# A macaron block with routed experts: quad addresses worked out together, and r projected from mixed rows

## What is computed

```python
x = x + 0.5 * ffn(layernorm(x))     # pass A
x = x + attn(layernorm(x))
x = x + 0.5 * ffn(layernorm(x))     # pass B
# ffn: shared swiglu of width 256, plus for each token the best 2 of 8 experts of width 128,
#      weighted by their normalised sigmoid scores
# attn:
xx = x shifted by one token
xk, xv, xr = (x * mix + xx * (1 - mix) for mix in (mix_k, mix_v, mix_r))
k, v, r = xk @ Wk.T, xv @ Wv.T, xr @ Wr.T
state_t = k_t * v_t + exp(time_decay) * state_(t-1)
o_t = r_t * (time_first * k_t * v_t + state_t)
out = layernorm(o) @ Wo.T
```

## Time and profile before

| | |
|---|---|
| median of 3 runs | 1294.95 us (1294.62 to 1298.04) |
| the profiled execution | 1293.77 us |
| its span, first to last instruction | 1291.5 us |
| mean granted TensorE clock | 0.916 of full speed |
| busy: TensorE, VectorE, GpSimd, ScalarE | 1042.8, 829.3, 714.7, 457.3 us |
| instructions | 28331 |

### The profile page before, as it was taken

How to read it: one execution, slowest core, us unless ns; L and a number is a source line. 1 busy time by engine, 2 the same in 40 slices (tenths; PEclk the granted TensorE clock), 3 DMA queues, 4 the chain that set the end, 5 groups by cost and what they waited for, 6 DMA issues and landing times.

```text
span 1291.5 us, 28331 instructions
## 1 busy us (share of the span) xinstructions
PE 1042.8 (81%) x8816; PEld 714.9 (55%) x8816; DVE 829.3 (64%) x2520; ACT 457.3 (35%) x819; POOL 714.7 (55%) x684
## 2 busy tenths in 40 slices
PE   1788699978898999789997979985899877698560
PEld 0466466744466666357664466755567444467450
DVE  5965668577779567766767854666576777642242
ACT  6334245422235444324432135342345223223230
POOL 2846752378873335777348781257842775530264
PEclk9989899997899999899997989997999988899795
DMA  9869985443375654469743577679744533477794
GB/s 289 222 122 211 243 163 131 98 121 98 119 151 104 164 128 144 142 142 211 168 136 110 163 149 171 155 205 183 181 107 132 143 110 90 118 154 170 185 262 131
DMA packets 340521, 201.00 MB, mean 156 GB/s; under 512 B 255904, under 2 KB 322592, under 8 KB 340256
## 3 DMA queue, kind: packets, MB, share of 16 engines
q1 hardware_dynamic: 314944, 131.94, 43.4%
q0 software_dynamic: 24576, 67.14, 20.4%
q10 hardware_dynamic: 864, 0.12, 0.1%
HBM read 47.05 MB, written 93.32 MB: 109 GB/s over the span
## 4 chain that ended last, share of the span: by engine, by line
POOL 30%; issue 22%; PE 20%; SPq 9%; DMA 8%; DVE 7%; ACT 3%; POOLq 0%; ACTq 0%; DVEq 0%
POOL y_got L800 13%; SPq L707 6%; POOL xsA L782 6%; POOL xsB L782 5%; PE ps L865 3%; PE ps L869 2%; PE ps L867 2%; DMA y_got<-ysA,y_pos 2%; DMA y_got<-ysB,y_pos 2%; POOL rstd L756 2%; PE ps L889 2%; POOL acc L808 2%; SPq L680 2%; POOL p_exp L773 2%; PE ps L891 1%
## 5 line engine op out<-in xcount | busy, mean ns | idle before, releaser
L865 PE MATMUL ps<-xq,w_hi 128*128 128x128 f16 x1280 | 263.3, 227 | 50.3 <-DMA xq<-xsB 28.1
L867 PE MATMUL ps<-xq,w_hi 128*128 128x128 f16 x1280 | 262.3, 227 | 0.0
L869 PE MATMUL ps<-xq,w_lo 128*128 128x128 f16 x1280 | 261.6, 226 | 0.0
L889 PE MATMUL ps<-wd_hi,hid_h 128*128 128x256 f16 (+1 forms) x576 | 164.2, 285 | 64.8 <-DVE hid_l L1213 29.5
L1234 DVE SCALAR_TENSOR_TENSOR acc<-y_got,share,acc 128x256 f32<-128x256 f32 x256 | 113.3, 484 | 136.0 <-DMA y_got<-ysB,y_pos 67.3
L800 POOL DMA_INDIRECT y_got<-ysB,y_pos x128 | 131.3, 1026 | 113.6 <-DMA ysB<-y_sb 70.6
L1095 ACT CAST hid_h<-hid 128x512 f16<-128x512 f32 x144 | 88.9, 619 | 294.7 <-DVE hid L1206 283.9
L782 POOL DMA_INDIRECT xsA<-rows,pos x128 | 137.2, 1072 | 97.7 <-DVE pos L1365 59.8
L865 PEld LDWEIGHTS ps<-xq,w_hi 128*128 x1280 | 129.5, 101 | 80.8 <-issue 62.4
L782 POOL DMA_INDIRECT xsB<-rows,pos x128 | 129.3, 1010 | 64.9 <-issue 35.6
L891 PE MATMUL ps<-wd_hi,hid_l 128*128 128x256 f16 (+1 forms) x576 | 164.9, 286 | 0.0
(11 more groups left out here) (150 smaller groups left out, 2218.0 us busy)
## 6 DMA issues: line engine op xcount, KB each, us to landing
ysA<-y_sb SPq DMA_DIRECT2D x40, 512.0 KB, 3.5
ysB<-y_sb SPq DMA_DIRECT2D x40, 512.0 KB, 3.6
acc<-in_x_dram SPq DMA_DIRECT2D x16, 512.0 KB, 5.3
out_dram<-acc SPq DMA_DIRECT2D x16, 512.0 KB, 3.5
xsA<-zeros SPq DMA_DIRECT2D x36, 128.0 KB
xsB<-zeros SPq DMA_DIRECT2D x36, 128.0 KB
acc<-in_w_chunks_dram SPq DMA_DIRECT2D x10, 384.0 KB, 8.5
xq<-xsA SPq DMA_TRANSPOSE x160
```

The source lines that it names most:

```text
L865: nc.tensor.matmul(half, w_hi[2 * k + b][:, cols], hi, start=(j == 0 and k == 0), stop=False, skip_group_check=True)
L867: nc.tensor.matmul(half, w_hi[2 * k + b][:, cols], lo, start=False, stop=False, skip_group_check=True)
L869: mm = nc.tensor.matmul(half, w_lo[2 * k + b][:, cols], hi, start=False, stop=(j == 3 and k == KC - 1), skip_group_check=True)
L889: nc.tensor.matmul(half, hid_h[:, b, tok], w_hi[DOWN][:, :, cols], start=(first and j % 2 == 0), stop=False, skip_group_check=True)
```

## The change

TensorE: ahead of a routed `gate_up`'s wait for its rows, the addresses of all weights of the quad's gate and up (four blocks, four w_hi and four w_lo) are worked out; the matmuls then use them. The addresses of `down` stay where they were. r's mix is no longer folded into its weights. ScalarE writes x * mix_r from the turned rows into r_sb (`r_part`), VectorE adds the shifted rows times 1 - mix_r (`r_mix`), both make the fp16 pair r_h, r_l (`mix_hi`, `mix_lo`), and `r_proj` multiplies it by plain W_r: 12 matmuls. r_sb also holds r later, so `r_part` waits for the previous sequence's `receive`. The planner gets the new tasks, other durations and other constants. In the set-up the weights of r are scaled once instead of four times. New semaphores (r_parted, r_mixed, mix_hi_done, mix_lo_done) count the new tasks; `project` is written more briefly for k and v, with the same matmuls.

```diff
@@ -70,7 +70,7 @@
-    WINDOW, FULL, BESIDE = 3.413, 0.75, 0.7
+    WINDOW, FULL, BESIDE = 3.413, 0.75, 0.9
...
@@ -210,16 +210,16 @@
-    FIRST_A = 17.1
-    FIRST_T = 114.3
-    A_LEAD = 223.9
-    A_GAP = 35.3
-    E_LEAD = 62.0
+    FIRST_A = 16.6
+    FIRST_T = 104.7
+    A_LEAD = 247.1
+    A_GAP = 32.8
+    E_LEAD = 40.2
...
-    EB_LAG = 14.6
-    E_GAP = 6.6
-    EB_GAP = 4.0
-    G_LAG = 93.4
+    EB_LAG = 5.0
+    E_GAP = 6.3
+    EB_GAP = 4.5
+    G_LAG = 135.3
...
@@ -274,7 +274,7 @@
-        add("pe", "gate_up", key, 3.3 if what == "E" else 2.75, at, after)
+        add("pe", "gate_up", key, 3.0 if what == "E" else 2.75, at, after)
...
-            add("sp", "fetch", (f, g, q), 5.9, at - 10 + gap * q,
+            add("sp", "fetch", (f, g, q), 5.7, at - 10 + gap * q,
...
@@ -323,8 +323,8 @@
-            add("act", "turn_hi", (s, m), 0.6, at + 9 + m, [("turn2", (s,))] + ([("r_proj", (s - N_XC,))] if s >= N_XC else []))
-            add("dve", "turn_lo", (s, m), 0.7, at + 10 + m, [("turn_hi", (s, m))])
+            add("act", "turn_hi", (s, m), 0.6, at + 9 + m, [("turn2", (s,))] + ([("kv_proj", (s - N_XC, KC - 1))] if s >= N_XC else []))
+            add("dve", "turn_lo", (s, m), 0.7, at + 10 + m, [("turn_hi", (s, m)), ("r_part", (s, m))])
...
-        add("pe", "r_proj", (s,), 5.3, at + 21, [("kv_proj", (s, KC - 1))])
+        for m in range(KC):
+            add("act", "r_part", (s, m), 0.6, at + 9.5 + m, [("turn2", (s,)), ("turn_hi", (s, m)), back("receive", s)])
+            add("dve", "r_mix", (s, m), 0.75, at + 14 + m, [("r_part", (s, m)), ("turn_lo", (s, m))])
+            add("act", "mix_hi", (s, m), 0.6, at + 15 + m, [("r_mix", (s, m)), back("r_proj", s)])
+            add("dve", "mix_lo", (s, m), 0.7, at + 16 + m, [("mix_hi", (s, m))])
+        add("pe", "r_proj", (s,), 2.65, at + 21,
+            [("kv_proj", (s, KC - 1))] + [("mix_lo", (s, m)) for m in range(KC)])
...
-        add("pool", "rstd_o", (s,), 0.75, at + 34, [("stats_o", (s,)), back("out_resid", s)])
+        add("pool", "rstd_o", (s,), 1.1, at + 34, [("stats_o", (s,)), back("out_resid", s)])
...
-        elif name == "turn_lo":
+        elif name == "r_mix":
...
@@ -477,11 +483,14 @@
-        a_hi = sb("a_hi", [P, 3, 2, KC, C], F16)
-        a_lo = sb("a_lo", [P, 3, 2, KC, C], F16)
+        a_hi = sb("a_hi", [P, 5, KC, C], F16)
+        a_lo = sb("a_lo", [P, 5, KC, C], F16)
+        r_h = sb("r_h", [P, KC, T], F16)
+        r_l = sb("r_l", [P, KC, T], F16)
...
-        mixing = sb("mixing", [P, 3, 2, KC])
+        mixing = sb("mixing", [P, 2, 2, KC])
+        less_mix = sb("less_mix", [P, KC])
...
@@ -627,7 +638,7 @@
-                return turn_lo_done, val("turn_lo", *key, b)
+                return r_mixed, val("r_mix", *key, b)
...
+                for j in range(4):
+                    for p in range(DOWN):
+                        for w in (w_hi, w_lo):
+                            nc.tensor.lower_ap(w[p][:, bass.ds(first[j], P)], for_matmul_weights=True)
...
@@ -982,9 +991,16 @@
                     project(s, bank, b, m).then_inc(done, 1)
             def r_proj(s):
+                pe.wait_ge(mix_hi_done, val("mix_hi", s, KC - 1))
+                pe.wait_ge(mix_lo_done, val("mix_lo", s, KC - 1))
                 for m in range(KC):
-                    bank = bank_free("r_proj", (s,), m)
-                    project(s, bank, 2, m).then_inc(r_done, 1)
+                    bank, cols = bank_free("r_proj", (s,), m), slice(m * P, (m + 1) * P)
+                    for k in range(KC):
+                        nc.tensor.matmul(ps[:, bank, :], a_hi[:, 4, k, cols], r_h[:, k, :], start=(k == 0), stop=False)
+                        nc.tensor.matmul(ps[:, bank, :], a_hi[:, 4, k, cols], r_l[:, k, :], start=False, stop=False)
+                        mm = nc.tensor.matmul(ps[:, bank, :], a_lo[:, 4, k, cols], r_h[:, k, :], start=False,
+                                              stop=(k == KC - 1))
+                    mm.then_inc(r_done, 1)
             def scan_turn(s):
                 pe.wait_ge(received, s + 1)
...
@@ -1068,13 +1084,13 @@
-                    act.wait_ge(mixing_done, 2)
-                    for which in range(3):
+                    act.wait_ge(mixing_done, 3)
+                    for which in range(2):
...
-                                ins = nc.scalar.activation(a_hi[:, which, part, k, :], a_stage[:, which, k, :], ACT.Copy,
-                                                           scale=mixing[:, which, part, k:k + 1])
-                    ins.then_inc(w_hi_done, 1)
+                                nc.scalar.activation(a_hi[:, 2 * which + part, k, :], a_stage[:, which, k, :], ACT.Copy,
+                                                     scale=mixing[:, which, part, k:k + 1])
+                    nc.scalar.activation(a_hi[:, 4], a_stage[:, 2], ACT.Copy, scale=W_SCALE).then_inc(w_hi_done, 1)
...
@@ -1125,9 +1141,22 @@
             def turn_hi(s, m):
                 act.wait_ge(turned2, 2 * s + m + 1)
                 if s >= N_XC:
-                    act.wait_ge(r_done, 2 * (s - N_XC + 1))
+                    act.wait_ge(v_done, 2 * (s - N_XC + 1))
                 nc.scalar.copy(xc_h[:, s % N_XC, m, :], ps[:, bank_of("turn2", (s,), m), :])\
                     .then_inc(turn_hi_done, 1)
+            def r_part(s, m):
+                act.wait_ge(turned2, 2 * s + m + 1)
+                if s > 0:
+                    act.wait_ge(received, s)
+                nc.scalar.activation(r_sb[:, m, :], ps[:, bank_of("turn2", (s,), m), :], ACT.Copy,
+                                     scale=chan[:, MIX_R, m:m + 1]).then_inc(r_parted, 1)
+            def mix_hi(s, m):
+                act.wait_ge(r_mixed, val("r_mix", s, m))
+                if s > 0:
+                    act.wait_ge(r_done, 2 * s)
+                nc.scalar.copy(r_h[:, m, :], r_sb[:, m, :]).then_inc(mix_hi_done, 1)
             def k_copy(s, m):
                 act.wait_ge(k_done, 2 * s + m + 1)
@@ -1139,8 +1168,7 @@
             def r_copy(s, m):
                 act.wait_ge(r_done, 2 * s + m + 1)
-                if s > 0:
-                    act.wait_ge(received, s)
+                act.wait_ge(mix_lo_done, val("mix_lo", s, KC - 1))
                 nc.scalar.activation(r_sb[:, m, :], ps[:, bank_of("r_proj", (s,), m), :], ACT.Copy,
                                      scale=W_UNSCALE).then_inc(r_copied, 1)
...
@@ -1421,11 +1449,27 @@
                     .then_inc(table_out, 1)
             def turn_lo(s, m):
                 dve.wait_ge(turn_hi_done, val("turn_hi", s, m))
+                dve.wait_ge(r_parted, val("r_part", s, m))
                 if s >= N_XC:
-                    dve.wait_ge(r_done, 2 * (s - N_XC + 1))
+                    dve.wait_ge(v_done, 2 * (s - N_XC + 1))
                 v.tensor_tensor(xc_l[:, s % N_XC, m, :], ps[:, bank_of("turn2", (s,), m), :],
                                 xc_h[:, s % N_XC, m, :], ALU.subtract).then_inc(turn_lo_done, 1)
+            def r_mix(s, m):
+                dve.wait_ge(r_parted, val("r_part", s, m))
+                dve.wait_ge(turned2, 2 * s + m + 1)
+                v.scalar_tensor_tensor(out=r_sb[:, m, 1:T], in0=ps[:, bank_of("turn2", (s,), m), 0:T - 1],
+                                       scalar=less_mix[:, m:m + 1], in1=r_sb[:, m, 1:T], op0=ALU.mult,
+                                       op1=ALU.add).then_inc(r_mixed, 1)
+            def mix_lo(s, m):
+                dve.wait_ge(mix_hi_done, val("mix_hi", s, m))
+                if s > 0:
+                    dve.wait_ge(r_done, 2 * s)
+                v.tensor_tensor(r_l[:, m, :], r_sb[:, m, :], r_h[:, m, :], ALU.subtract).then_inc(mix_lo_done, 1)
             def kv(s, m):
                 dve.wait_ge(k_copied, 2 * s + m + 1)
...
@@ -1484,9 +1528,10 @@
-            v.tensor_scalar(mixing[:, :, 0, :], chan[:, MIX_K:MIX_R + 1, :], W_SCALE, None, ALU.mult)\
+            v.tensor_scalar(less_mix[:], chan[:, MIX_R, :], -1.0, 1.0, ALU.mult, ALU.add).then_inc(mixing_done, 1)
+            v.tensor_scalar(mixing[:, :, 0, :], chan[:, MIX_K:MIX_R, :], W_SCALE, None, ALU.mult)\
...
-            v.tensor_scalar(mixing[:, :, 1, :], chan[:, MIX_K:MIX_R + 1, :], -W_SCALE, W_SCALE, ALU.mult, ALU.add)\
+            v.tensor_scalar(mixing[:, :, 1, :], chan[:, MIX_K:MIX_R, :], -W_SCALE, W_SCALE, ALU.mult, ALU.add)\
```

More of the change, by code:

```diff
@@ L956, in project @@
                 cols, n = slice(m * P, (m + 1) * P), s % N_XC
[L957 to L961, removed]
-                                     skip_group_check=True)
-                    nc.tensor.matmul(ps[:, bank, :], a_lo[:, which, 0, k, cols], hi, start=False, stop=False,
-                                     skip_group_check=True)
-                for k in range(KC):
-                    hi, lo = xc_h[:, n, k, 0:T - 1], xc_l[:, n, k, 0:T - 1]
-                    nc.tensor.matmul(ps[:, bank, 1:T], a_hi[:, which, 1, k, cols], hi, start=False, stop=False,
```

(27 more changed lines are left out.)

7 lines of the change are left out of this document (5 added, 2 removed).

## The result

The changed kernel takes 1226.03 us, median of 4 runs (1221.58 to 1227.36), beside 1295.15 of the kernel before: ratio 0.9456, 95% interval [0.9427, 0.9485], or 69 us less. The forecast was 1247, its range 1208 to 1280. The total lies in the range, but by luck: how it comes about does not answer to the sum, as the experiments show.

What follows compares the result with a forecast made beforehand. TensorE, 87% busy in the body, was taken as the bound where dense, with a fetch-bound tail. Gains of 31 (r), 16 (addresses) and 6 (order) less 6 (VectorE) made 47 us off 1293.8: forecast 1247, range 1208 to 1280.

Steps and rivals of the forecast that it cites:

- what it saves there, the span saves: Reading of the stage from 400 to 500 us, TensorE busy 95.5 of 100: its saving there shortens the span.
- r, 24 matmuls to 12: r_proj in 16 sequences: 41 us less TensorE, counted whole in eight dense sequences and half in eight, 31 us gain.
- Addresses: Routed gate_ups: address block about 1.0 us per quad, slow quads become fast, four fifths passed on, 16 us gain.
- VectorE's added work: r_mix and mix_lo, 46 us on VectorE, delay gated and hidden_lo: 6 us loss, bounds 0 and 16.
- The added waits: turn_lo waits for r_part, which waits for the previous receive, so kv_proj comes behind that receive: costed at nothing.
- The order: Planner's new leads, gaps and durations reorder all queues: 6 us gain, bounds 20 either way, about three longest waits.
- The tail: Last routed quads, 190 us: bound by SyncE's transposed fetches, not products; quads still start 6.3 us apart.
- everything passes: Rival: TensorE is the bound wherever over 80% busy and other tasks fill waits; 1212 us, chance 0.18.
- Other queues hold it: Rival: GpSimd's and SyncE's queues hold the span, only dense stretches gain, about a third; 1275 us, chance 0.15.
- The clock takes it back: Rival: TensorE with less to do shows a lower clock, 0.90 instead of 0.93 in the body; 1271 us, chance 0.03.
- Slower, as addresses are not cheaper in a block: Rival: block addresses cost 0.115 us each, 3.7 us per quad without a matmul; 1318 us, chance 0.07.

Runs made afterwards that it cites:

- after's order: The engines' task queues as the planner makes them for the changed kernel itself, which takes 1226.03 us.
- old_work_new_order: Work of the kernel before, run in the changed kernel's queues with r's four steps taken out: 1243.97 us, 0.9609 to the kernel before.
- addr_rmix: Kernel before with the address block, r from mixed rows and its planner tasks, constants and other durations as before: 1311.85 us, 1.0144 to the kernel before.
- jitter: Changed kernel with the planner constant FIRST_T at 104.6 instead of 104.7, same instructions in another order: 1266.03 us, 0.9792 to the kernel before.
- after_light: Changed kernel, same order, with r_mix and mix_lo on 2 columns instead of 512 behind the first sequence: 1219.65 us, 0.9404 to the kernel before.
- after_down: Changed kernel, same order, with the addresses of down's weights in the block too: 1220.48 us, 0.9441 to the kernel before.

## Why the prediction came out as it did

The forecast gave 1247 and the time is 1226. Its sign and its range hold, and the TensorE time that each part saves was right; that the total lies in the range is luck. The step that failed is the first one, in the reading of the bound: "what it saves there, the span saves". The terms 31 and 16 rest on it, and the runs show 3 to 11 us of the end for some 40 us of TensorE by the addresses and 6 ± 5 us for 35 us of it by r's matmuls. The second is the order, put at 6 us.

- **r, 24 matmuls to 12 (forecast 31, bounds 21 and 41).** TensorE's saving was right: 40 us measured, 41 worked out. The value was not: 6 ± 5 us in after's order. I passed on everything in eight sequences and half in the rest, but a dense stage showed an engine that was present (matmul spans overlap) rather than one that held the end.
- **Addresses (forecast 16, bounds 0 and 27).** The mechanism was right: packing, a block of 0.80 us against 1.0, slow gate_ups gone, 42 us of TensorE. Passing on four fifths was wrong; it is 3 to 11 us, inside the bounds. ("3.9 us at most" for a quad's products leaves out two of the tail at the low clock, 4.4 and 5.0 us; both are still under the 6.3 of the fetches.)
- **VectorE's added work (forecast 6 of loss).** Measured 7 ± 8 us for a little over half of it. The interval reaches from nothing to more than twice the forecast, so it neither confirms the size nor refutes it.
- **The added waits (nothing).** kv_proj now waits 9.3 us in 7 places, each time until 0.1 us behind turn_lo's end; in old_work_new_order its line has 3.3 us. The new wait of turn_lo for r_part isn't the reason. In all seven places r_part had ended 0.8 to 5.0 us before turn_lo started, and VectorE was at other tasks ahead of it in its queue, or waited for them, and went from the last of them into turn_lo without a gap: for sequence 3, the one with 3.7 us, r_part ends at 337.7 and turn_lo starts at 342.7, behind additions of gathered rows that came late. So the zero for this wait holds there; what the 6 us of TensorE cost in the end was not tried alone.
- **The order (forecast 6 of gain, bounds 20 either way).** This is the term that carries the result: 30 ± 4 us for the constants in the old task list, 51 ± 7 for after's queues with the old work, far outside the bound. The bound, "three of the longest waits", was the wrong yardstick: it looked at TensorE's waits alone, where a single wait of GpSimd in the tail had 61.0 us. Which waits the order removed is known only in part, as said above.
- **The tail.** I had quads 6.3 us apart; SyncE now issues five in 29.5 us, 5.9 each, since no store stands between. The tail is 20 us shorter, 18 of them with the old work in the new order.

So the errors cancelled in part: 47 forecast as 41 of work (31 + 16 - 6) and 6 of order, against some 20 of work and 51 of order. Of the rivals, "everything passes" (1212) is 14 us off for a wrong reason: nearly nothing passes. "Other queues hold it" (1275) came nearest in mechanism, but still let the dense stretches pass on, and gave the order nothing of its own. "The clock takes it back" did not come about in this change (0.921 beside 0.916); the clock was lower in orders in which TensorE waits more: 0.895 with the new work in the old order, 0.886 in addr_rmix, 0.900 in jitter. "Slower, as addresses are not cheaper in a block" is refuted by the 0.80 us.

**What stays open.** Measured one by one in after's order the parts give 5 + 6 - 7 = 4 us, together 20 ± 8; in the old order all together give -2 ± 3. The gap between the two is 15 ± 13 us, barely clear of noise, though after_light took away only a part of VectorE's work, and the whole of it would widen the gap. It may be that each part alone is still covered by the other's absence, or that old_work_new_order suffers where other waits of the old program (turn_hi's for r_proj, r_copy's for receive) meet queues made for the new one. No run tells these apart. Nor was r's part tried in the old order with its steps at other places, or down without its eight computations.

## What to carry to other kernels

Where several engines run fixed queues and meet at semaphores, a busy share of 87% or even 95% on one is no proof that its time is the span's. Price a saving by an experiment that takes it away in the unchanged order, and look for the longest single wait on every engine, not only on the busiest. A change that also regenerates the order is two changes: run each work in the other's order before crediting either, and treat the constants of such a planner as something to be searched by timing on the chip, since a tenth of a microsecond in one of them was worth 40 us here. And look in the trace whether an experiment did what its edit says: after_down computed its addresses ahead and then again.

## What had not been expected of the hardware

Register computations next to each other are packed far better than the earlier trace rows let one think: 32 addresses became six instructions of 74 ns, 0.1325 us apart, 0.80 us for the block, or 0.025 us for each against 0.115 us for a computation between matmuls. And with TensorE's time freed in a fixed order its granted clock was lower: 0.895 with the whole new work in the old order (0.886 to 0.900 in ten runs) beside 0.916 before (0.912 to 0.923 in the thirteen runs beside them). With the same work in the new order it is 0.921: here it depended on where the waits lie, not only on how much work there is.
